# Four-layer attention chain on one core: VectorE adds the last two partial sums of the exponentials, and the denominators take one group of matmuls a block

## The reference

```python
# layer 0 (head dimension 16, a position bias, layer norm behind it)
attn = jnp.einsum('bhdi,bhdj->bhij', q * scale, k) + pos[..., :, None] + pos[..., None, :]
y = jnp.einsum('bhij,bhdj->bhdi', jax.nn.softmax(attn, axis=-1), v)
# layers 1 and 2 (head dimension 32, group norm ahead of them)
scores = jnp.einsum('bhqd,bhkd->bhqk', q * scale, k)
o = jnp.einsum('bhqk,bhkd->bhqd', jax.nn.softmax(scores, axis=-1), v)
```

## Time and profile before

| what | us |
|---|---|
| median of 3 runs | 469.26 (469.04, 469.26, 471.65) |
| the profiled execution | 470.91 |
| its span, in the profile | 469.2 |
| outside the span | 1.7 |
| TensorE busy in the span | 435.7 (93%) |
| VectorE busy | 368.4 (79%) |
| ScalarE busy | 258.5 (55%) |
| GpSimd busy | 215.0 (46%) |

### The profile page before, as it was taken

The page is one execution under the profiler, slowest core; times in us unless marked ns, Lnnn a source line. Parts: engine busy times, 40 slices in busy tenths (PEclk is TensorE's granted clock), DMA queues, the critical chain, the costliest instruction groups (busy, mean ns, idle before and its releaser), DMA issues.

```text
span 469.2 us, 7016 instructions
## 1 busy us (share of the span) xinstructions
PE 435.7 (93%) x2210; PEld 241.2 (51%) x2210; DVE 368.4 (79%) x748; ACT 258.5 (55%) x515; POOL 215.0 (46%) x195
## 2 busy tenths in 40 slices
PE   8888999999896899999899999989999999998996
PEld 6544555554255475555445333657555455532463
DVE  7699998985777599997788486579998787848663
ACT  3238777775613337876677561224786676763032
POOL 8300031428010007899989911002799889971000
PEclk9989999999898999999999989999999999999998
DMA  5331545003300265589943530045378954550002
GB/s 158 52 69 25 159 67 134 23 5 68 70 0 0 58 146 113 125 181 193 212 105 61 112 68 3 1 108 128 79 165 173 198 110 81 110 96 25 0 1 89
DMA packets 20476, 41.87 MB, mean 89 GB/s; under 512 B 7278, under 2 KB 8566, under 8 KB 20184
## 3 DMA queue, kind: packets, MB, share of 16 engines
q1 hardware_dynamic: 15144, 25.41, 21.6%
q0 software_dynamic: 5152, 16.00, 18.4%
q10 hardware_dynamic: 144, 0.02, 0.0%
HBM read 8.30 MB, written 1.12 MB: 20 GB/s over the span
## 4 chain that ended last, share of the span: by engine, by line
PE 64%; DVE 14%; ACT 5%; POOL 4%; DMA 4%; SPq 4%; issue 3%; ACTq 0%; DVEq 0%; POOLq 0%
PE banks L1046 15%; PE banks L1035 14%; PE banks L1006 13%; DVE max L755 7%; PE banks L978 6%; DMA k_stack<-kL 4%; ACT E L610 3%; POOL SUMS L546 3%; DVE SUMS L784 3%; PE banks L1173 3%; PE banks L952 2%; PE banks L1061 2%; SPq L360 2%; SPq L353 2%; PE banks L1207 2%
## 5 line engine op out<-in xcount | busy, mean ns | idle before, releaser
L755 DVE TENSOR_REDUCE max<-banks 128x1 f32<-128x512 f32 x384 | 239.4, 683 | 32.9 <-PE banks L1006 32.0
L610 ACT ACTIVATE E<-banks 128x512 f32<-128x512 f32 x384 | 200.6, 616 | 44.3 <-PE banks L1035 42.0
L546 POOL TENSOR_TENSOR SUMS<-E 128x512 f32<-128x512 f32 x120 | 159.0, 1501 | 106.6 <-ACT E L610 106.5
L1006 PE MATMUL banks<-k_stack,q_stack 126*128 126x512 f32 x384 | 163.3, 439 | 8.5 <-DMA k_stack<-kL 6.2
L1035 PE MATMUL banks<-q_stack,k_stack 128*128 128x512 f32 x384 | 154.6, 413 | 5.7 <-ACT E L610 5.6
L1006 PEld LDWEIGHTS banks<-k_stack,q_stack 126*128 126x128 f32 x384 | 72.7, 191 | 44.4 <-DVE max L755 11.9
L1035 PEld LDWEIGHTS banks<-q_stack,k_stack 128*128 128x128 f32 x384 | 72.5, 191 | 41.6 <-ACT E L610 20.2
L1046 PE MATMUL banks<-E,V 128*32 128x512 f32 x768 | 93.6, 609 | 0.0
L1046 PEld LDWEIGHTS banks<-E,V 128*32 128x32 f32 x768 | 21.0, 111 | 47.5 <-issue 25.8
L599 ACT ACTIVATE mHL<-banks 8x128 fp32r<-8x128 f32 x48 | 12.7, 264 | 49.3 <-PE banks L1025 49.3
L521 POOL TENSOR_TENSOR att<-pv_sb,rec_sb 128x512 f32<-128x512 f32 x9 | 13.8, 1529 | 46.4 <-DMA rec_sb<-rec_rows 46.4
(11 more groups left out here) (149 smaller groups left out, 316.7 us busy)
## 6 DMA issues: line engine op xcount, KB each, us to landing
SUMS<-SUMS POOLq DMA_DIRECT2D x30, 512.0 KB, 4.9
k_stack<-kH SPq DMA_DIRECT2D x28, 128.0 KB, 2.3
q_stack<-qH SPq DMA_DIRECT2D x40, 64.0 KB, 2.0
rec_sb<-rec_rows SPq DMA_DIRECT2D x9, 256.0 KB
q_stack<-qH SPq DMA_DIRECT2D x16, 128.0 KB, 2.8
k_stack<-kL SPq DMA_DIRECT2D x14, 128.0 KB, 4.1
k_stack<-kH SPq DMA_DIRECT2D x22, 64.0 KB, 2.3
q_stack<-qL SPq DMA_DIRECT2D x20, 64.0 KB, 2.0
```

The lines of the kernel that those rows point to most:

```text
L546: pool.tensor_tensor(SUMS[:, slot, :], E[:, E_PLAN[s][0], :], E[:, E_PLAN[s + 1][0], :], ALU.add).then_inc(sum_ready, 1)
L610: act.activation(E[:, slot, :], B[:, ring_of_scores(l, s) % B_RING, :], ACT.Exp, scale=1.0 if l == 0 else float(HEAD_DIM[l]) ** -0.5).then ...
L755: dve.tensor_reduce(max8[:, m % 2, 2 * t + half:2 * t + half + 1], A[:, A_PLAN[l][i][0], :], AX.X, ALU.max).then_inc(a_used, 1)
L1006: pe.matmul(A[:, bank, :], q_stack[0:SHIFT_ROW, slot, q0:q0 + P], k_stack[0:SHIFT_ROW, slot, k0:k0 + HALF], start=True, stop=True).then_in ...
```

## The change

- For units 0 to 11 of layers 1 and 2, VectorE adds the two sums that are left, result 1 onto result 0 (`merge_sums`), at step 8j + 22 (one step earlier for unit 11). It waits for the unit's accumulating DMA.
- `denominators` runs once a block with four matmuls over the one sum of each unit, and waits for the merges of the block. Its steps are 51, 83 and 112 in place of 49, 81 and 111.
- The slots of SUMS are laid out anew: eight slots for result 0, four for result 1, two pairs for results 2 and 3. Results 0 and 1 of a unit no longer lie side by side, and so the destination of the accumulating DMA is two pieces of 2 KB on each partition with a gap between them, where it was one piece of 4 KB.
- GpSimd's waits follow: for result 0 on the denominators of the block from eight units before, for result 1 on the merge of the unit four before.
- Y, the row of layer 0 and the last reciprocals get other slots; the wait for the late position rows moves from SyncE's load of Y to GpSimd's first result 1 of layer 0. VectorE's first sum of units 14 and 15 waits for the denominators of block 1 in place of block 2.

```diff
-SUM_UNITS = 6
-SUM_SLOTS = 2 * SUM_UNITS + 4
+SUM_UNITS = 8
+SUM_SLOTS = 2 * SUM_UNITS
...
-DEN_STEPS = (49, 81, 111)
+DEN_STEPS = (51, 83, 112)
+MERGED_UNITS = 12
...
 def sum_slot(j, k):
-    return 2 * (j % SUM_UNITS) + k if k < 2 else 2 * SUM_UNITS + 2 * (j % 2) + k - 2
+    return (j % SUM_UNITS, SUM_UNITS + j % 4, SUM_UNITS + 4 + 2 * (j % 2), SUM_UNITS + 5 + 2 * (j % 2))[k]
+
+
+def merge_step(j):
+    return TILES * j + 22 - (j == MERGED_UNITS - 1)
+
+
+MERGED_AT = {merge_step(j): j for j in range(MERGED_UNITS)}
...
-        last_rec = SUMS[:, 5, :]
+        last_rec = SUMS[:, 10, :]
...
-        Y = SUMS[:, 8:12, :].rearrange("p a (b c) -> p (a b) c", c=C)
-        row0_sb = SUMS[:, 0, 0:C]
+        Y = SUMS[:, 0:4, :].rearrange("p a (b c) -> p (a b) c", c=C)
+        row0_sb = SUMS[:, 4, 0:C]
...
                 if l == 0:
-                    for late in pos_late:
-                        sp.wait_ge(late, 16 * POS_ROWS)
                     sp.dma_start(Y, xt).then_inc(xt_in, 16)
...
-                        if k < 2 and j >= SUM_UNITS and l:
-                            pool.wait_ge(den_done, den_groups(l, (j - SUM_UNITS) // HEADS_B, k))
+                        if k == 0 and j >= SUM_UNITS and l:
+                            pool.wait_ge(den_done, den_groups(l, (j - SUM_UNITS) // HEADS_B))
+                        elif k == 1 and j >= 4 and l:
+                            pool.wait_ge(merged, MERGED_UNITS * (l - 1) + j - 3)
                         elif k < 2 and l:
                             pool.wait_ge(den_done, den_groups(l - 1, BLOCKS - 1))
+                        elif k == 1:
+                            for late in pos_late:
+                                pool.wait_ge(late, 16 * POS_ROWS)
...
-                    kept, added = sum_slot(j, 0), sum_slot(j, 2)
-                    pool.dma_start(SUMS[:, kept:kept + 2, :], SUMS[:, added:added + 2, :],
+                    kept, other, added = sum_slot(j, 0), sum_slot(j, 1), sum_slot(j, 2)
+                    pool.dma_start(SUMS[:, kept:other + 1:other - kept, :], SUMS[:, added:added + 2, :],
                                    accum_op=ALU.add).then_inc(sum_dma[j % 2], 16)
...
                 elif l:
-                    dve.wait_ge(den_done, den_groups(l, BLOCKS - 2))
+                    dve.wait_ge(den_done, den_groups(l, 1))
...
+            def merge_sums(l, j):
+
+                dve.wait_ge(sum_dma[j % 2], dma_count(l, j))
+                dve.tensor_tensor(SUMS[:, sum_slot(j, 0), :], SUMS[:, sum_slot(j, 0), :], SUMS[:, sum_slot(j, 1), :],
+                                  ALU.add).then_inc(merged, 1)
...
+                    if l and s in MERGED_AT:
+                        merge_sums(l, MERGED_AT[s])
...
-            def denominators(l, b, k):
+            def denominators(l, b):
 
                 bank, first = den_bank(l, b), HEADS_B * b
-                if k == 0 and b < DENS_IN_RING[l]:
+                if b < DENS_IN_RING[l]:
                     ring_free(l, ring_of_den(l, b))
-                elif k == 0:
+                else:
                     pe.wait_ge(a_used, STEPS * (l + 1))
-                pe.wait_ge(sum_dma[0], dma_count(l, first + 2))
-                pe.wait_ge(sum_dma[1], dma_count(l, first + 3))
+                pe.wait_ge(merged, MERGED_UNITS * (l - 1) + HEADS_B * (b + 1))
                 for u in range(HEADS_B):
-                    mm = pe.matmul(bank[DP * u:DP * (u + 1), :], ones[:, 0:DP], SUMS[:, sum_slot(first + u, k), :],
-                                   start=(k == 0), stop=(k == 1))
+                    mm = pe.matmul(bank[DP * u:DP * (u + 1), :], ones[:, 0:DP], SUMS[:, sum_slot(first + u, 0), :],
+                                   start=True, stop=True)
                 mm.then_inc(den_done, 1)
...
                     if l and s in DEN_STEPS:
-                        denominators(l, DEN_STEPS.index(s), 0)
-                        denominators(l, DEN_STEPS.index(s), 1)
+                        denominators(l, DEN_STEPS.index(s))
```

More of the change, by code:

```diff
@@ L202, in attention_chain @@
         sum_dma = [sem(f"sum_dma{i}") for i in range(2)]
-        unit_sums, obias_set = sem("unit_sums"), sem("obias_set")
+        unit_sums, merged, obias_set = sem("unit_sums"), sem("merged"), sem("obias_set")
         pv_out, den_out = sem("pv_out"), sem("den_out")
@@ L268, in den_groups @@
         def den_groups(l, b, k=1):
-            return 2 * BLOCKS * l + 2 * b + k + 1 - 2 * (BLOCKS - 1)
+            done = l and 2 + (BLOCKS + 1) * (l - 1)
+            return done + ((BLOCKS - 1 if l else 0) + k if b == BLOCKS - 1 else b) + 1
         def dma_count(l, j):
```

## The result

Four runs of the changed kernel gave 498.68 to 510.24 us, median 505.33, against 469.15 for the kernel before: a ratio of 1.068 (95% interval 1.063 to 1.073). Medians here are of all runs and ratios of the fast runs alone, which for this set are 498.68 and 504.30, mean 501.5. In a second set on the chip it gave 509.43 against 469.98, 1.082 (1.076 to 1.088). The loss is thus 32 us in the first set and 39.5 in the second, where the forecast, 479.1, had 9.8. The profiled execution took 498.68, of it 496.9 in the span.

The account below looks back on a forecast made before the run. Three engines run nearly level, TensorE setting the time; after the change GpSimd would be late: 9.0 - 1.93 - 2.19 = 4.9 us a layer, 9.8 on 469.26, giving 479.1 us. Range 467 to 492.

Parts of the forecast that it names:

- TensorE's saving: Denominator matmuls halved in three blocks of two layers: 5.6 us, taken as hidden behind late GpSimd.
- GpSimd's slack: Units 2 to 13: 1.93 us idle plus 2.19 before ScalarE's step 118, 4.1 a layer, against 9.0 of growth.
- The DMA issue: GpSimd's accumulating DMA with two pieces a partition: 0 to 0.39 us more each, 0.19 taken, 2.3 a layer.
- VectorE's room: 11.3 us idle a layer would hold 12 additions of 0.69, 8.3 by themselves; with waits, 1 us a layer over.
- The path that the sum priced: ScalarE at step 118 waits for GpSimd's multiplication behind unit 13: 4.9 us a layer, 9.8 together, covering VectorE's 1 us.
- the sign named for the rival: TensorE's score matmuls for the maxima mainly waiting for VectorE would show that VectorE had lost its turn.
- The hold: Each merge delays GpSimd by 0.24 to 0.69 us; 0.56 taken, 6.7 us a layer for 12 merges.
- The hand-over: VectorE's merge waits for a running GpSimd sum: 0.5 us if fair, 1.56 at the other end; 0.6 taken.
- VectorE loses its turn: Rival: GpSimd's queued sum goes first, merges take 2.25 us, 11.6 a layer: 492.5, or 485 to 488; chance 0.2.
- The merge never waited for its DMA: Rival: GpSimd falls behind, VectorE's last two or three merges wait for the DMA, 2 to 3 us each: 487; chance 0.1.
- The saving did not arrive: Rival: GpSimd absorbs the merges and fewer denominator matmuls pay: 466.9, or 463.7 if GpSimd is no bound; chance 0.12.
- nothing cancelled: Rival: GpSimd delayed about 0.34 to 0.5 us a merge, DMA no dearer: between 469 and 473 us; chance 0.18.

Follow-up runs that it names:

- The one-input operations: Kernel before plus 24 unused VectorE maxima of one 128x512 SBUF tile at the merges' steps: 474.54 us against 468.86, ratio 1.010.
- the kernel with slots side by side: Changed kernel with results 0 and 1 adjacent again, DMA in one piece: 477.97 us; with its merges moved two steps earlier, 496.01 us.
- merges at step 24: Changed kernel, split DMA kept, merges two steps later at 8j + 24 (unit 11 still at 109): 494.70 us, ratio 1.053.
- the kernel at step 20: Changed kernel with results 0 and 1 adjacent, DMA in one piece, and merges at step 8j + 20: 496.01 us against 468.86, ratio 1.055.
- the one that leaves a part of the sum out: Kernel before with four denominator matmuls a block over result 0 alone, no merge, DMA in one piece: 467.34 us against 468.86, ratio 0.996.
- Two kernels with the same total of merge time: Changed kernel in the second set, 509.43 us; and changed kernel with GpSimd waiting before unit j's third sum for unit j - 2's merge, 495.55 us.

## Why the prediction was wrong, point by point

**TensorE's saving.** Right as a part of the sum: it was counted as worth nothing behind GpSimd, and 1.5 us is all it brings with nothing else changed.

**GpSimd's slack.** Nearly right. The split DMA alone used it up, with 32% of the chain on GpSimd and the waits at `pv_sb` that had been named, but 1.2 to 1.4 us a layer came through where 4.0 taken from 4.1 should have left nothing. The DMA issue cost 0.33 where half the bound, 0.19, was taken; undersized by 3.4 us in all.

**VectorE's room.** Wrong in kind. The prediction let 11.3 us of idle hide 8.3 us of work. The one-input operations, which took 0.67 to 0.69 each whatever GpSimd did, cost 5.7 us. The idle was there in sum and hid only a part; no run shows which of it a merge could have used.

**The path that the sum priced.** Wrong for the changed kernel. All 9.8 us were to come from ScalarE at step 118, waiting for GpSimd's late multiplication, with VectorE's share "covered". In the changed kernel that wait is absent in layers 1 and 2:

```profile
289.28 0.62 ACT L629 ACTIVATE pv_sb<-banks 128x512 f32<-128x512 f32 x1
```

GpSimd had idles of up to 3.37 us there, its units came 6.5 to 9.9 us apart and not 6.8 to 7.1, and the sign named for the rival came instead: the scores for the maxima wait for VectorE, 65.0 us. With the DMA in one piece the changed program takes 477.97, close to the forecast of 479.1, but without the forecast's wait there either: 5.7 and 4.0 us on VectorE's side, less 1.5 saved. That agreement is luck. The hold itself was sized rightly: four sums with a merge in between take 5.91 us against 5.30, 0.6 where 0.56 was taken.

**The hand-over: the step that failed.** "I take 0.6, near the fair end, since the addition at 115.08 met an ordinary sum, as a merge will, and waited for its rest alone, while that at 269.93 met a DMA issue". The addition at 115.08 met the last sum of a unit, which has no sum queued behind it. A merge meets the third, often with the fourth ready behind it, and is then passed as the addition at 269.93 was. The mean wait came out at 0.9 to 1.1 us, not 0.6. The second fault of the step was to price by the mean, and so to find VectorE only 1 us a layer over its room. The merges that were passed take 2.6 to 3.0 us, up to 5.1 in the second set; the four banks cover about 1 us of each by the prediction's own estimate, and the rest stops TensorE. The rival "VectorE loses its turn" had the mechanism; it was given 0.2, its 492.5 was toned down with the argument that GpSimd's idles would let VectorE in, and the range was cut there.

**What no rival had: the clock.** The granted clock fell from 0.983 to 0.966 in the profiled run and to 0.951 in the second set's. Span times the missing share is 8.0 us before, 16.9 and 24.7 after; taken off, the spans are 461.2 before and 480.0 and 479.3 after. So the spans' growth of 27.7 and 34.8 us is 18 to 19 that would be there at full clock, and 9 and 17 of half speed. The second part is an upper bound, since it takes TensorE to set the time in all of those stretches. Not all of that can come from the merges, since a part stands ahead of the first of them. The first 175 us of the kernel before, the changed one, and the changed one in the second set (clock third from the end):

```profile
0.00:175.00 175.00, 157.53 (x775) 92.83 (x776) 141.77 (x289) 91.48 (x176) 40.97 (x49) 0.97 0.29 68
0.00:175.00 175.00, 157.29 (x768) 93.95 (x769) 140.00 (x284) 90.25 (x174) 41.44 (x49) 0.95 0.28 67
0.00:175.00 175.00, 158.60 (x761) 94.67 (x762) 139.20 (x282) 90.25 (x174) 41.66 (x49) 0.93 0.28 66
```

That is some 3.5 and 7 us of the 9 and 17, which leaves at most 5.5 and 10 behind stalls in the layers with merges. Why layer 0 has less clock in these two profiles is open. The 18 to 19 lie between the forecast's 9.8 and the rival's 23.2.

**The other rivals.** The merge never waited for its DMA: the view of L802 has no idle before it. The saving did not arrive, and nothing cancelled.

The rule of the Trainium skill (SBUF — State Buffer, "Who interferes with whom"), that the one who starts first holds the pair, would have given 0.5 us a merge; the eight merges that asked ahead of the sum that passed them go with the row of 269.93 instead.

**Accounts.** Against 469: saving -1.5; split DMA 3 to 6; VectorE's work 5.7; the shared port at a good place 4.0: 480 to 483. The remaining 18 to 29 us to 501.5 and 509 come with the place of the merge, but for what the lower clock ahead of the first merge costs (unit 0's DMA is issued 1.6 and 3.2 us later in the two profiles). That a place makes the loss is shown (18 us in the kernel with slots side by side); the other way it mended 7 to 15 and not all of it. Two things are open. One is how the 1.4 to 1.5 us merges at step 24 still cost what they do. The other is how much the clock adds: the kernel at step 20, whose merges are longer in sum (51.7 against 38 to 43 us), had 0.981 in its profile and 0.964 to 0.983 over its runs, against 0.939 to 0.966 for the changed kernel.

No version tried is faster than the kernel before beyond the one that leaves a part of the sum out, and that by 0.4%.

## What to carry to other kernels

Before VectorE is given an operation with two SBUF inputs beside a busy GpSimd, read in the timeline what GpSimd has queued behind the instruction that the operation will meet, and take that whole length as the price, with one input as the cheap alternative. Price a stall by its longest case against the buffers that cover it, and then ask what TensorE's clock does after it. When slots are moved, look at whether a DMA's pieces stay whole: 0.33 us an issue was small by itself, and yet it set GpSimd further behind ScalarE, where the next sum is ready when a merge asks.

## What was unexpected of the hardware

- A VectorE addition with two SBUF inputs that asks first can be passed by a GpSimd sum that starts later (211.73 against 212.61). It was passed in all 17 cases in which that sum's input had been ready for 0.25 us or more when the running one ended, and in none of the 53 with 0.19 or less. It ends about 0.56 us after the last sum that it had to let through; the 17 took 2.6 to 3.1 us.
- Splitting each partition's 4 KB destination into two pieces took GpSimd's DMA issue from 0.87 to 1.20 us, a third of a microsecond for 128 more pieces; the packets of its queue went from 5152 to 8992.
- Two kernels with the same total of merge time, 43 us, differ by 14 us, with a granted clock of 0.983 and 0.951. In the faster one the merges are more even; that this is the cause is not shown.
